# Deformable convolution on one core: whole spread rounds ahead of four gathers

## What is computed

```
x = x + L0_conv(gn(x))
x = x + L1_conv(gn(x))

om = conv3x3(x, w_om) + b_om
dy, dx = om[:, 0:18:2], om[:, 1:18:2];  mask = sigmoid(om[:, 18:])
ys = dy + ky + row - 1;  xs = dx + kx + column - 1
vals = bilinear(x, ys, xs) * mask
out = einsum('bckhw,ock->bohw', vals, weight) + bias
```

## Time and profile before

| | us |
|---|---|
| median of 3 runs | 2084.99 |
| lowest, highest | 2080.31, 2085.33 |
| profiled execution, its time | 2089.32 |
| profiled execution, its span | 2087.3 |
| TensorE busy | 1872.2 (90%) |
| VectorE busy | 1381.8 (66%) |
| ScalarE busy | 1156.3 (55%) |
| POOL busy | 880.5 (42%) |

### The profile page before, as it was taken

How to read it: one execution, slowest core, us unless ns; L and a number is a source line. 1 busy time by engine, 2 the same in 40 slices (tenths; PEclk the granted TensorE clock), 3 DMA queues, 4 the chain that set the end, 5 groups by cost and what they waited for, 6 DMA issues and landing times.

```text
span 2087.3 us, 187708 instructions
## 1 busy us (share of the span) xinstructions
PE 1872.2 (90%) x83517; PEld 1448.2 (69%) x83517; DVE 1381.8 (66%) x2326; ACT 1156.3 (55%) x2378; POOL 880.5 (42%) x1153
## 2 busy tenths in 40 slices
PE   8565347799999999999999999999999999999986
PEld 3321035577777777877777777777777777778774
DVE  8779524466666666666666666666666666666663
ACT  0003244466666666666666666666666666666652
POOL 1000023355555555555555554545555555555440
PEclk9689759999999999999999999999999999999998
DMA  9025641223333333333333333333323323333320
GB/s 354 1 95 210 274 146 53 58 79 82 83 83 84 83 84 84 84 84 84 84 84 84 82 82 84 84 84 84 81 79 82 81 80 83 83 84 84 84 70 12
DMA packets 161698, 196.28 MB, mean 94 GB/s; under 512 B 20288, under 2 KB 136672, under 8 KB 157536
## 3 DMA queue, kind: packets, MB, share of 16 engines
q1 hardware_dynamic: 161632, 195.34, 31.7%
HBM read 143.05 MB, written 52.22 MB: 94 GB/s over the span
## 4 chain that ended last, share of the span: by engine, by line
PE 64%; issue 11%; ACT 11%; DVE 8%; DMA 2%; DVEq 2%; SPq 1%; POOL 0%; ACTq 0%; POOLq 0%
PE pE L1005 18%; PE pVV L1080 14%; PE pVV L1026 11%; PE pM L1047 9%; PE pR L1035 8%; ACT big L599 5%; ACT big L594 5%; PE pM L1057 4%; DVE big L736 3%; DMA xh_scratch<-win 1%; DVE big L769 1%; DVEq L736 1%; DMA win<-xh_scratch 1%; DVE big L763 1%; DVE stats L671 1%
## 5 line engine op out<-in xcount | busy, mean ns | idle before, releaser
L502 POOL COPY big<-win 128x480 f32<-128x480 f32 x520 | 289.1, 586 | 865.8 <-DMA win<-xh_scratch 553.1
L490 POOL TENSOR_TENSOR prod<-big 128x600 f32<-128x600 f32 (+1 forms) x489 | 504.2, 1040 | 0.0
L763 DVE COPY big<-pE 128x768 f32<-128x768 f32 x390 | 368.8, 946 | 192.5 <-PE pE L1005 192.3
L1026 PE MATMUL pVV<-big 60*32 60x72 f32 x33280 | 470.2, 231 | 23.0 <-issue 21.3
L1026 PEld LDWEIGHTS pVV<-big 60*32 60x32 f32 x33280 | 374.9, 106 | 130.4 <-issue 124.2
L1005 PE MATMUL pE<-big,sel_s 32*64 32x96 f32 x24960 | 415.2, 255 | 22.8 <-issue 11.2
L1005 PEld LDWEIGHTS pE<-big,sel_s 32*64 32x64 f32 x24960 | 342.2, 132 | 80.1 <-issue 53.0
L758 DVE COPY big<-pVV 128x288 f32<-128x288 f32 x520 | 230.8, 444 | 228.3 <-PE pVV L1026 224.9
L769 DVE STREAM_TRANSPOSE big<-prod 128x768 f32<-128x768 f32 x390 | 377.7, 968 | 5.6 <-POOL prod L490 5.2
L1035 PE MATMUL pR<-ident,big 128*128 128x128 f32 x2080 | 346.5, 290 | 18.6 <-ACT big L599 1.4
L599 ACT ACTIVATE big<-pR 128x512 f32<-128x512 f32 x520 | 311.0, 598 | 43.4 <-PE pR L1035 42.9
(11 more groups left out here) (75 smaller groups left out, 1162.0 us busy)
## 6 DMA issues: line engine op xcount, KB each, us to landing
big<-xh_scratch SPq DMA_DIRECT2D x390, 136.0 KB
win<-xh_scratch SPq DMA_DIRECT2D x130, 408.0 KB, 3.7
xh_scratch<-win SPq DMA_DIRECT2D x32, 544.0 KB, 2.7
big<-in_x SPq DMA_DIRECT2D x16, 1024.0 KB, 15.8
x_scratch<-big SPq DMA_DIRECT2D x16, 1024.0 KB, 3.8
x1r<-x_scratch SPq DMA_DIRECT2D x256, 64.0 KB, 3.1
out<-outs SPq DMA_DIRECT2D x256, 64.0 KB, 2.1
xh_scratch<-zero SPq DMA_DIRECT2D x4, 204.0 KB, 2.7
```

Source lines behind the costliest of these rows:

```text
L490: made = nc.gpsimd.tensor_tensor(prod[:, kx, at:at + m, 0:SQ].rearrange("p m (a b) -> p m a b", a=NSH), hy.to_broadcast(shape), hx.to_broa ...
L502: last = nc.gpsimd.tensor_copy(strips[:, half * HTP:(half + 1) * HTP, h, 0:REG].rearrange("p t (r x) -> p t r x", r=WIN_R), tiles_of(q, h, ...
L763: nc.vector.tensor_copy(*both_units(j, 2)).then_inc(e_dve, 1)
L1026: last = mm(o[:, :, t * TILE_C:(t + 1) * TILE_C, :], XT[part, x:x + C], A[part, at, :], start=True, stop=True)
```

## The change

A round now is one kx for all 16 tile pairs: 16 matmuls of 192 columns instead of 32 of 96. All three rounds of a set come first, with the convolve of the set before and the offsets of a later set between them; then four gathers, with the turn_rows of the next set between. ScalarE copies its half of a round in one instruction of 768 columns instead of two of 384. On VectorE, ScalarE and POOL the steps are written in the new order, and straight code ahead of the loop ends three steps earlier on TensorE, ScalarE and POOL.

```diff
-HSLOT = IPG * HTP
-UNIT = ROWS * HSLOT
-
-ROUND_OF = (((0, 0), (0, 1)), ((0, 2), (1, 0)), ((1, 1), (1, 2)))
+VGROUPS = [(0, 4), (4, 8), (8, 12), (12, 16)]
+NG = len(VGROUPS)
...
-                peeled(at, g * NSET + 5)
-                at = looped(g * NSET + 5, ((g + 1) * NSET if apart else SETS) - 3, g)
+                peeled(at, g * NSET + (5 if apart else 2))
+                at = looped(g * NSET + (5 if apart else 2), ((g + 1) * NSET if apart else SETS) - 3, g)
...
+        def expanded(kx, h):
+
+            src = pE[:, h * 1024:(h + 1) * 1024].rearrange("p (a n) -> p a n", a=2)[:, :, 0:EPX]
+            dst = A.rearrange("p n (r a m) -> p r a n m", r=ROUNDS, a=QUADS)
+            return dst[:, kx, 2 * h:2 * h + 2], src.rearrange("p a (m n) -> p a n m", n=SLOT)
...
             def step(N, s, on, place):
                 if on[1]:
                     cut_tiles(N + 1, 1 - s % 2, 0)
-                    product(N + 1, (s + 1) % RING, 0)
-                    cut_tiles(N + 1, 1 - s % 2, 1)
                     product(N + 1, (s + 1) % RING, 1)
+                    product(N + 1, (s + 1) % RING, 2)
...
+                    product(N + 2, (s + 2) % RING, 0)
                 if on[1]:
-                    product(N + 1, (s + 1) % RING, 2)
+                    cut_tiles(N + 1, 1 - s % 2, 1)
...
+                for k in range(TCH):
+                    if on[0] and k < NG:
+                        samples(N, k)
+                    if on[1] and k < TCH - 1:
+                        turned(N + 1, k)
...
+                if on[0]:
+                    table(N, 0)
+                if on[1]:
+                    turn(N + 1, 0)
                 if on[-1]:
-                    samples(N - 1, 2)
+                    output(N - 1, 1 - s % 2, place)
+                if on[0]:
+                    table(N, 1)
+                if on[1]:
+                    turn(N + 1, 1)
                 if on[2]:
-                    dve.wait_ge(msk_done, N + 3)
-                    wait(dve, lin_done, N + 2)
-                    wait(dve, reach_done, N + 2)
+                    dve.wait_ge(abs_done, N + 3)
+                    nc.vector.tensor_tensor(reach[:, :], U.rearrange("p (m k) -> p m k", k=NSH)[:, :, REACH],
+                                            reach[:, :], ALU.max).then_inc(reach_done, 1)
+                if on[0]:
+                    table(N, 2)
+                if on[1]:
+                    turn(N + 1, 2)
+                if on[0]:
+                    samples(N, 0)
+                if on[3]:
+                    dve.wait_ge(msk_done, N + 4)
+                    wait(dve, lin_done, N + 3)
+                    wait(dve, reach_done, N + 3)
...
+                    for gi in range(1, NG):
+                        samples(N, gi)
...
-            def spread(n, j):
-
-                pe.wait_ge(pt_done, n * KS + (2, 3, 3)[j])
-                wait(pe, e_act, n * ROUNDS + j)
-                wait(pe, e_dve, n * ROUNDS + j)
-                for c, (half, kx) in enumerate(ROUND_OF[j]):
-                    for i2 in range(TILE_R):
-                        for h, u in itertools.product(range(2), range(QUADS)):
-                            part = slice(u * BLK, (u + 1) * BLK)
-                            t0 = h * NTP + half * HTP
-                            src = PT[part, kx, :].rearrange("p (m b t) -> p m b t", m=ROWS, b=IPG)
-                            o = pE[h * HALF:(h + 1) * HALF, u * 512 + c * UNIT:u * 512 + (c + 1) * UNIT] \
-                                .rearrange("p (m b t) -> p m b t", m=ROWS, b=IPG)
-                            last = mm(o[:, i2::TILE_R], sel_s[part, i2 * KS + kx, :],
-                                      src[:, i2::TILE_R, :, t0:t0 + HTP], start=True, stop=True)
+            def spread(n, kx):
+
+                pe.wait_ge(pt_done, n * KS + (kx + 1))
+                wait(pe, e_act, n * ROUNDS + kx)
+                wait(pe, e_dve, n * ROUNDS + kx)
+                for i2 in range(TILE_R):
+                    for h, u in itertools.product(range(2), range(QUADS)):
+                        part = slice(u * BLK, (u + 1) * BLK)
+                        src = PT[part, kx, :].rearrange("p (m b t) -> p m b t", m=ROWS, b=IPG)
+                        o = pE[h * HALF:(h + 1) * HALF, u * 512:u * 512 + EPX] \
+                            .rearrange("p (m b t) -> p m b t", m=ROWS, b=IPG)
+                        last = mm(o[:, i2::TILE_R], sel_s[part, i2 * KS + kx, :],
+                                  src[:, i2::TILE_R, :, h * NTP:(h + 1) * NTP], start=True, stop=True)
                 last.then_inc(e_done, 1)
 
...
+            def gather(n, gi):
+
+                t0, t1 = VGROUPS[gi]
+                if gi == 0:
+                    pe.wait_ge(e_act, n * ROUNDS + ROUNDS)
+                    pe.wait_ge(e_dve, n * ROUNDS + ROUNDS)
                     wait(pe, conv_read, n)
-                wait(pe, v_act, n * TCH + k)
-                wait(pe, v_dve, n * TCH + k)
+                pe.wait_ge(xt_done, n * TCH + (t1 + TPC - 1) // TPC)
+                wait(pe, v_act, n * NG + gi)
+                wait(pe, v_dve, n * NG + gi)
...
             def step(N, s, on, place):
-                if on[-1]:
-                    gather(N - 1, 2)
                 if on[0]:
                     spread(N, 0)
-                    turn_rows(N, 2)
-                if on[-1]:
-                    gather(N - 1, 3)
-                if on[0]:
-                    turn_rows(N, 3)
-                    spread(N, 1)
                 if on[-1]:
                     convolve(N - 1)
+                if on[0]:
+                    spread(N, 1)
                 if on[3]:
                     offsets(N + 3)
                 if on[0]:
-                    gather(N, 0)
                     spread(N, 2)
-                if on[1]:
-                    turn_rows(N + 1, 0)
-                if on[0]:
-                    gather(N, 1)
-                if on[1]:
-                    turn_rows(N + 1, 1)
+                    turn_rows(N, 3)
                 if on[3]:
                     turn_offsets(N + 3)
+                for k in range(TCH):
+                    if on[0] and k < NG:
+                        gather(N, k)
+                    if on[1] and k < TCH - 1:
+                        turn_rows(N + 1, k)
```

More of the change, by code:

```diff
@@ L627, in step @@
                 if on[0]:
[L628 removed]
                     table(N, 2)
[L630 to L635 removed]
+                    turned(N, 3)
                 if on[3]:
@@ L753, in _, with samples, table @@
             dve.wait_ge(xh_done, N_XH * g_count)
-            def samples(n, k):
-                dve.wait_ge(v_done, n * TCH + (k + 1))
-                nc.vector.tensor_copy(*evacuate(k, 1)).then_inc(v_dve, 1)
-            def table(n, j):
-                dve.wait_ge(e_done, n * ROUNDS + (j + 1))
-                nc.vector.tensor_copy(*both_units(j, 2)).then_inc(e_dve, 1)
+            def samples(n, gi):
+                dve.wait_ge(v_done, n * NG + (gi + 1))
+                nc.vector.tensor_copy(*evacuate(gi, 1)).then_inc(v_dve, 1)
+            def table(n, kx):
+                dve.wait_ge(e_done, n * ROUNDS + (kx + 1))
+                nc.vector.tensor_copy(*expanded(kx, 1)).then_inc(e_dve, 1)
             def turn(n, kx):
                 dve.wait_ge(prod_done, n * KS + (kx + 1))
-                wait(dve, e_done, (n - 1) * ROUNDS + (2, 3, 3)[kx])
+                wait(dve, e_done, (n - 1) * ROUNDS + (kx + 1))
                 nc.vector.transpose(PT[:, kx, :], prod[:, kx, :, :].rearrange("p m k -> p (m k)")) \
@@ L803, in step @@
                 if on[0]:
-                    turn(N, 2)
-                    table(N, 0)
-                if on[-1]:
-                    samples(N - 1, 3)
-                if on[0]:
-                    table(N, 1)
-                if on[-1]:
-                    output(N - 1, 1 - s % 2, place)
-                if on[1]:
-                    turn(N + 1, 0)
-                if on[2]:
-                    dve.wait_ge(abs_done, N + 3)
-                    nc.vector.tensor_tensor(reach[:, :], U.rearrange("p (m k) -> p m k", k=NSH)[:, :, REACH],
-                                            reach[:, :], ALU.max).then_inc(reach_done, 1)
-                if on[0]:
-                    samples(N, 0)
-                    table(N, 2)
-                if on[1]:
-                    turn(N + 1, 1)
-                if on[0]:
-                    samples(N, 1)
+                    for gi in range(1, NG):
+                        samples(N, gi)
             steps(dve, step, 2, True)
@@ L1019, in gather @@
                 pe.nop(nofuse=True)
-                for t in range(TPC):
+                for t in range(t0, t1):
                     for b, h in itertools.product(range(IPG), range(2)):
                         part = slice(h * HALF, h * HALF + REG)
-                        at = half * HSLOT + b * HTP + k % 2 * TPC + t
```

(9 more changed lines are left out.)

60 lines of the change are left out of this document (15 added, 45 removed).

## The result

The changed kernel takes **2132.3 us** (median of 4 runs, 2131.4 to 2134.4); the kernel before, timed beside it, 2083.7 (2080.3 to 2085.3). The ratio is 1.024, with a 95% interval of 1.022 to 1.025. The forecast was 1978 and faster; this is 2.4% slower, outside the range of 1925 to 2060.

A forecast was written before the change was run, and what follows sets the result against it. TensorE's queue, almost without holes, was taken as the bound. 124 sets x 0.53 = 66, plus 27 and 14 from straight code, made 107 us off 2085.0: 1978 us, range 1925 to 2060.

The forecast's parts named there:

- Spread: TensorE's three rounds of 192-column matmuls: each takes 0.80 us instead of 0.97, a gain of 0.51 per set.
- the first rival: Columns bind the spread, which stays at 0.97; a set takes 13.13 and the kernel 2042 us; chance 0.20.
- Waits that go: TensorE's 0.45 us of waiting per set, at turn_rows and at spreads behind late table copies, goes as a whole.
- Wait of a gather for the one before: Each gather waits until the previous one's samples are copied out of the same banks: 0.13 us, three times a set.
- Wait of the first gather for the tables: The first gather needs all three tables and waits 0.04 us for round 2's copy, ends 0 and 0.2.
- 3 x 0.80 + 9.79 + 0.04 + 3 x 0.13: One set on TensorE, spreads, other groups and new waits: 12.62 us against 13.15, 0.53 less.
- Queues passed: Reordered work on VectorE, ScalarE and POOL, and SP's DMAs, stays covered and is priced at nothing.
- tables of rounds 0 and 1: Waits of the next spread for these rounds' table copies are hidden, round 1's with 0.2 us to spare.
- Straight code: Fewer instructions to load outside the loop: 27 us saved at the start and 14 at the tail, 41 together.
- the second rival: Stops at both ends are not made by the straight code's length; the 41 us stay: 2019 us; chance 0.06.
- The third rival: Gathers are bound by their copies and the spread gets no cheaper: 13.77 a set, 2121 us; chance 0.07.

The follow-up runs named there:

- Experiments 1 to 4: Changed kernel with both sample copies halved: 2074.0 us; only VectorE's halved: 2073.4; only ScalarE's: 2130.0; first three gathers in the spread's PSUM banks: 2061.0.
- experiment 6: Changed kernel with the first gather's two waits for the table copies written behind its other four waits: 2112.0 us.
- experiment 8: Changed kernel with gathers in the spread's banks, TensorE's loop beginning with the gathers, and the table waits behind the first gather's other wait: 1968.3 us.
- experiment 5: Changed kernel with TensorE's loop pass beginning with the gathers, so the jump lies ahead of the first gather, matmul order the same: 2086.2 us.
- experiment 9: Kernel before with only the straight code ahead of the loop cut from eight steps to five on engines other than VectorE: 2068.0 us against 2084.9.
- experiments 1 and 4: Changed kernel with both sample copies halved: 2074.0 us; with the first three gathers in the spread's PSUM banks: 2061.0 us.

## Why the prediction was wrong

- **Spread: right.** It was priced at 0.80, from convolve's cost per column and the wider weights, and came out at 0.84, far from the 0.97 of the first rival. No run shows whether the weights are what makes it more than 0.73.
- **Waits that go: right.** In the changed kernel turn_rows follows a gather after 0.81 and no round waits for the table copy of the round before it in the loop (0.84, 0.83).
- **Wait of a gather for the one before: right in kind, too small.** The term took 0.13 from a release of 0.15; that was the release from a table copy to a spread. It is 0.25 from VectorE's sample copy to a gather, so the wait is 0.23. In one of three it is 0.30, just beyond the upper end of 0.29: there the copy starts 0.99 and not 0.92 behind its gather (1004.98 to 1005.97), and why is open. Together that is 0.37 a set more than forecast, 46 us. Experiments 1 to 4 show it: with VectorE's copy shorter or the banks apart, the pitch follows.
- **Wait of the first gather for the tables: mis-sized, beyond its ends.** 0.04 was forecast, 0.2 at most; it is 0.36 (1.05 against 0.69), 40 us. The copy itself is only 0.10 later than worked out: spread to copy's end is 1000.98 to 1002.95, 1.97, against 0.80 + 0.11 + 0.96 = 1.87. What was late is the gather, 0.40 behind the copy. In the loop that lag is longer when other waits are written behind the one that ends last: moving the tables' two behind them gives 0.16 back (experiment 6), and with fewer waits as well nearly all (experiment 8, 0.75). In straight code it is 0.10 with the old order (experiment 6).
- **The step that failed outright is the sum of a set, "3 x 0.80 + 9.79 + 0.04 + 3 x 0.13".** It has no term for the loop's jump. Before, the jump stood between turn_offsets and a gather, in the 0.69 of the earlier trace rows, where it costs nothing: in the straight code of the kernel before, where there is no jump, the distance is 0.69 as well (315.33 to 316.02):

```profile
315.33 0.76 PE L1057 MATMUL pM<-perm_s,om_s 128*128 128x108 f32 x6
316.02 0.89 PE L1026 MATMUL pVV<-big 60*32 60x72 f32 x64
```

  The change moved it between the fourth gather and the first spread, and there it costs 0.38, 47 us. That is the largest of the four differences, by little; putting it back alone (experiment 5) makes the kernel as fast as the one before. Why it is free at one place and not at the other stays open.
- **Queues passed, tables of rounds 0 and 1: right.** The four differences above leave no room for another wait in the loop. Only in the tail, where no offsets lie between, round 2 waits 1.21 for round 1's copy, in three steps:

```profile
2071.64 0.91 PE L984 MATMUL pE<-big,sel_s 32*64 32x192 f32 x32 [1.21 <-DVE big L745]
```

- **Straight code: right in kind, 25 instead of 41.** The stops are made by its length (experiment 9 shortens it alone), so the second rival falls. The start gave 18.4 (20.6 with the work done ahead) and not 27. Between the stops at 318.81 and 359.68 there are 1,127 records, 40.87 us or 4.57 for 126, not 4.07. Part of it is the clock: from 340 to 360 us the mean granted clock is 0.76, and one convolve that takes 2.25 in the loop took 4.09.

```profile
342.32 4.09 PE L1059 MATMUL pVV<-big,wc 64*32 64x128 f32 x144
```

```profile
340.00:360.00 20.00, 16.72 (x534) 12.13 (x519) 8.83 (x13) 8.23 (x14) 7.15 (x11) 0.76 0.21 58
```

The tail gave 6.4 and not 14; the wait above stands in it three times, 3.6 us, and the rest was not taken apart.

The third rival had the waits nearly right, 1.07 a set where about 1.12 was measured (0.23 + 0.30 + 0.23 + 0.36). It held that the spread must stay at 0.97 as well for the time to get worse; the spread got cheaper by 0.40 a set, and the jump took 0.38 of that back. That its 13.77 a set and 2121 us come so near to the 13.76 and 2132 is luck. The Trainium skill, "TensorEngine Tiling (Array Packing)", PSUM Bottleneck, warned of the copies, and experiments 1 and 4 agree: the pitch falls from 1.63 to 1.47 with half the copy and to 1.40 with none in the way. With all three of the misjudged costs taken out, the same order takes 12.46 a set, where the forecast's work without its waits is 3 x 0.80 + 9.79 = 12.19; so the work was priced about right, and what stood between the pieces of work was not. That its 1968 us lie close to the 1978 of the forecast is in part chance: it has no waits between gathers at all, which the forecast had at 0.39 a set, and it gains about 30 us and not 41 at the two ends (2087.3 - 1966.0 by the spans, less 124 x 0.74).

## What to carry to other kernels

Before reordering a queue, write down for each boundary between two groups what else stands there: the loop's jump, the number and order of the waits, the engine whose copy lets go. A distance read from a trace is only good for that boundary with all that stands in it. Where the same banks are filled and emptied in turn, put other work or other banks between, and try the jump of the loop at another boundary: that is a small edit, and here it was worth 46 us.

## What was not expected of the hardware

- The loop's jump on TensorE costs 0.38 us behind a gather of 64 short matmuls, 0.56 with two more waits behind it, and nothing behind turn_offsets (0.69 with and without it in the kernel before).
- VectorE's copy lets a gather go 0.25 us after its end by the profile, ScalarE's after 0.16 or less; why VectorE's is slower towards a gather than towards a spread (0.15) stays open.
- The order in which waits are written counts in the loop: 0.16 us for two of them. In straight code the gather came 0.10 behind the copy with the order unchanged.
- "Issue" in the profile can be a wait for a copy (1.63 fell to 1.47 with the copy), and a named copy can be a jump (0.48 "from ScalarE" went when the jump alone was moved).
- A loop body of 2,168 matmuls and weight loads on TensorE takes 42.4 us a pass, where two passes of one with 1,084 take 24.9.
